# A power moved ahead of a selection, three more zero products, and K begun on the upper part of the context

## The chip, the cores and the metric

The kernel runs on one core of a Trainium2 chip. The metric is the device time of an execution in microseconds (us); before the change the median of three runs is 744.03 us. Names used: TensorE (PE), its weight loads (PEld), VectorE (DVE), ScalarE (ACT), GpSimd (POOL), SyncE (SP), which only issues DMAs.

## The reference

For 32 batches of `x` and `ctx`, each 64 channels by 512 positions, in float32:

```python
q, k, v = layernorm(x), ctx, ctx
qh, kh, vh = Wq q, Wk k, Wv v              # 8 heads of 64 channels, 512 positions
qh = softmax(qh, over channels) / 8 ; kh = softmax(kh, over positions)
context = kh vh^T ; out = context^T qh ; out = Wo out + bo
x = x + out / max(norm(out, over channels), 1e-12) * g * 8

xf = layernorm(x)                          # 2048 rows of 512
inter = xf c1^T c2^T                       # 1792 columns, 56 blocks of 32
idx = argmax in each block
h = relu(w1[idx] . xf)                     # one of 32 per block
x = x + sum over blocks of h * w2t[idx]
```

## The kernel before

One program covers both halves. Each engine has its own list of instructions, written out by hand as functions; their order on an engine is the order of the calls, and between engines they wait for each other by semaphore counts. Float32 operands of the products are split into an upper part (`_hi`, `_high`) and a rest (`_lo`, `_low`), so that a product is three terms: upper by upper, and twice upper by rest.

**The attention** takes one batch per step, `step(g, ...)` for g from -1 to 33. On TensorE a step has `keys(0)`, `keys(1)` (K's two halves, line 1300, into `slot[0]` and `slot[1]`), the products with V (line 1274) and with Q (line 1277) of the batches before, `queries(0)`, `queries(1)` (line 1314, into the same slots) and transposes of E and Q. VectorE takes the maxima (`max_k` line 784, `max_q` line 750) and shifts Q (`shift_q`, line 759); ScalarE takes the exponentials and copies.

The **start** is the step g = -1 and the step g = 0. On TensorE the step -1 is `zeros(12)`: products of a tile of zeros (line 1214), into a bank that nothing reads. On SyncE `ctx[0]` is loaded first. ScalarE rounds it into `c_high[0]` (line 1022, counts `c_hi`), VectorE subtracts into `c_low[0]` (line 804, counts `c_ready`). `keys(0)` waits for `c_ready` and for `wk_lo`. The terms of `keys` go n = 0, 1, 2: (`wk_hi`, `c_high`), (`wk_lo`, `c_high`), (`wk_hi`, `c_low`), two products each. In step 0 `keys(1)` is followed by `fold_vo()` (line 1075, waits for `wv` and `woT`), `zeros(4)`, a wait for small loads, `queries(0)`, `zeros(5)`, `queries(1)`, which waits for the exponential of K's second half. VectorE in that time: `split_wk`, `c_low`, `statistics(0)` (lines 767 and 769), `max_k(0)`, `split_first_x` (lines 773 to 778; its last, `x_low`, is what `queries(0)` waits for), `max_k(1)`, `max_q(0)`, `shift_q(0)`, `statistics(1)`, `max_q(1)`, `shift_q(1)`.

**The second half** takes rows in pairs of 128-row tiles ("duos", d = 0 to 7). A duo has 8 uses, u = 0 to 7: four chunks of `inter`'s columns (256, 512, 512, 512 wide; u // 2 is the chunk) by two tiles (u % 2). For one use: `project(d, u)` on TensorE (line 1129); `block_max(d, u)` on VectorE (lines 640 and 645: block maxima, and a mask of the places that reach them); `rank_mask(d, u)` on GpSimd (line 451); `first_max(d, u)` on VectorE (line 653); `select(d, u)` on GpSimd (line 464, writes `behind`); and then on SyncE the transposes of `behind`, 128 by 128 each (`turn_mask`, line 293: two for a use of the first chunk, four for the others). Seven pairs of 128 hidden columns, i = 0 to 6, use the transposed masks: `hide(d, i)` on TensorE (line 1147, 24 products), `gate(d, i)` on VectorE (line 663; for i = 1 and 2 it waits for the transposes of u = 2 and u = 3, so twelve in all stand ahead of `gate(0, 1)`), `h_high(d, i)` on ScalarE (line 928), `h_low(d, i)` on VectorE (line 669), `down(d, i)` on TensorE (line 1165, 12 products, waits for `h_low(d, i)`).

In the same duo the next two tiles, a = 2d + 2 and a + 1, are prepared: `norms(a)` on VectorE (lines 596 and 598: sums of squares per channel group, into `norm`), `invert(a, 2)` on GpSimd (line 423: their power -1/2, for both tiles), `turn_factors(a, 2)` on TensorE (line 1097, waits for `invert`), `exchange(d)` on ScalarE (line 886 copies the factors, line 892 stores them, line 898 issues four DMAs that load them spread over the channels), `scale` (line 602), `residual` (609), `moments_of` (614, 616) and `normalize` (621) on VectorE with `prepare` on GpSimd (408, 412) between, and `turn_x(a)`, `turn_x(a + 1)` on TensorE (line 1106).

The order around the change in the first pair is, on TensorE from `duo(0)`: `hide(0, 1)`, `turn_factors(2, 2)`, `project(0, 6)`, `hide(0, 2)`, `down(0, 0)`, `project(0, 7)`, `down(0, 1)`, `hide(0, 3)`, `turn_x(2)`, `turn_x(3)`, `hide(0, 4)`. On VectorE: `first_max(0, 2)`, `norms(2)`, `norms(3)`, `block_max(0, 4)`, `gate(0, 0)`, and from `duo(0)`: `first_max(0, 3)`, `h_low(0, 0)`, `first_max(0, 4)`, `block_max(0, 5)`, `first_max(0, 5)`, `gate(0, 1)`, `block_max(0, 6)`, `h_low(0, 1)`, `gate(0, 2)`, then `scale`, `residual` and `moments_of` for both tiles and `normalize(2)`, `first_max(0, 6)`, `normalize(3)`. On GpSimd: `select(0, 2)`, `rank_mask(0, 4)`, and from `duo(0)`: `select(0, 3)`, `invert(2, 2)`, `rank_mask(0, 5)`, `select(0, 4)`, `select(0, 5)`, `rank_mask(0, 6)`, `prepare(2)`, `prepare(3)`.

Of the kernel before, what the change touches and what calls it, by code (L numbers as in the profile page):

```python
# [81 lines left out]
def program(nc, A, scratch, factors, out):  # L82
    with ExitStack() as ctx:
# [150 lines left out]
        with nc.Block() as block:  # L234
# [164 lines left out]
            def _(pool):  # L399
# [19 lines left out]
                def invert(a, w):  # L419
                    pool.wait_ge(norm_max, a + w)  # L420
                    if a > 1:
                        pool.wait_ge(inv_turned, a // 2 + 1)
                    nc.gpsimd.tensor_tensor(inv[:, a % 2:a % 2 + w], norm[:, a % 2:a % 2 + w],
                                            neg_half[:].unsqueeze(2).broadcast_to([P, w, 2 * NT]),
                                            ALU.pow).then_inc(norm_inv, 1)
# [18 lines left out]
                def rank_mask(d, u):  # L444
                    use, w = USES * d + u, CHUNKS[u // 2][1]
                    if use == 0:
                        pool.wait_ge(rank_done, 1)
                    pool.wait_ge(i_mask, use + 1)
                    if later(use - 1):
                        pool.wait_ge(i_sel, use - 1)  # L450
                    nc.gpsimd.tensor_tensor(blocks(ranked[u % 2][:, 0:w]), blocks(mask[u % 2][:, 0:w]),  # L451
                                            rank[:].unsqueeze(1).broadcast_to([P, w // SPARSE, SPARSE]),
                                            ALU.mult).then_inc(i_ranked, 1)

                def select(d, u):
                    use, w = USES * d + u, CHUNKS[u // 2][1]
                    pool.wait_ge(i_first, use + 1)
                    if use in (0, 2):
                        pool.wait_ge(q_turned, HT * (B - 1 + use // 2))
                    if u >= 4:  # L460
                        pool.wait_ge(mask_in[u - 4], 16 * (CHUNKS[(u - 4) // 2][1] // P) * (d + 1))
                    elif later(d):
                        pool.wait_ge(mask_in[u + 4], 16 * (CHUNKS[(u + 4) // 2][1] // P) * d)
                    nc.gpsimd.tensor_tensor(blocks(behind[use % 4][:, 0:w]), blocks(ranked[u % 2][:, 0:w]),  # L464
                                            spread(first[u % 2][:, 0:w // SPARSE], w // SPARSE),
                                            ALU.subtract).then_inc(i_sel, 1)

                def duo(d, last):
                    select(d, 3)
                    if not last:  # L470
                        invert(2 * d + 2, 2)
                    rank_mask(d, 5)
                    select(d, 4)
                    select(d, 5)
                    rank_mask(d, 6)
                    if not last:
                        prepare(2 * d + 2)
                        prepare(2 * d + 3)
                    select(d, 6)
                    rank_mask(d, 7)  # L480
                    select(d, 7)
                    if not last:
                        begin(d + 1)

                def begin(d):
                    rank_mask(d, 0)
                    rank_mask(d, 1)
                    select(d, 0)
                    rank_mask(d, 2)
                    select(d, 1)  # L490
                    rank_mask(d, 3)
                    select(d, 2)
                    rank_mask(d, 4)

                def step(g, k, par, known):
# [87 lines left out]
            def _(dve):  # L583
# [7 lines left out]
                def norms(a, bank):  # L591
                    t = a % 2
                    dve.wait_ge(squared, a + 1)
                    if later(a - 1):
                        dve.wait_ge(norm_inv, inverted(a - 2))
                    nc.vector.tensor_reduce(by_factor(norm[:, t]), by_pair(bank[:]), AX.X, ALU.add).then_inc(norm_sum, 1)
                    dve.wait_ge(norm_sum, a + 1)
                    nc.vector.tensor_scalar(norm[:, t], norm[:, t], NORM_EPS * NORM_EPS, None, ALU.max).then_inc(norm_max, 1)
# [49 lines left out]
                def first_max(d, u):  # L648
                    use, w = USES * d + u, CHUNKS[u // 2][1]
                    dve.wait_ge(i_ranked, use + 1)  # L650
                    if later(use - 1):
                        dve.wait_ge(i_sel, use - 1)
                    nc.vector.tensor_reduce(first[u % 2][:, 0:w // SPARSE], blocks(ranked[u % 2][:, 0:w]), AX.X,  # L653
                                            ALU.max).then_inc(i_first, 1)
# [23 lines left out]

                def duo(d, last):
                    a = 2 * d + 2  # L680
                    first_max(d, 3)
                    h_low(d, 0)
                    first_max(d, 4)
                    block_max(d, 5)
                    first_max(d, 5)
                    if d:
                        result_of(2 * d - 2)
                        result_of(2 * d - 1)
                    gate(d, 1)
                    block_max(d, 6)  # L690
                    h_low(d, 1)
                    gate(d, 2)
                    if not last:
                        for t in range(2):
                            scale(a + t)
                            residual(a + t)
                            moments_of(a + t)
                        normalize(a)
                    first_max(d, 6)
                    if not last:  # L700
                        normalize(a + 1)
                    block_max(d, 7)
                    if not last:
                        xT_rest(a, pre[0])
                        xT_rest(a + 1, pre[1])
                    h_low(d, 2)
                    first_max(d, 7)
                    gate(d, 3)
                    gate(d, 4)
                    if not last:  # L710
                        z_low(d + 1)
                    h_low(d, 3)
                    if not last:
                        block_max(d + 1, 0)
                        block_max(d + 1, 1)
                        first_max(d + 1, 0)
                    h_low(d, 4)
                    if not last:
                        block_max(d + 1, 2)
                        first_max(d + 1, 1)  # L720
                        block_max(d + 1, 3)
                    gate(d, 5)
                    if not last:
                        first_max(d + 1, 2)
                    gate(d, 6)
                    if not last:
                        block_max(d + 1, 4)
                    if d + 2 < DUOS:
                        norms(a + 2, pre[0])
                    h_low(d, 5)  # L730
                    if d + 2 < DUOS:
                        norms(a + 3, pre[1])
                    h_low(d, 6)
                    if not last:
                        gate(d + 1, 0)
# [125 lines left out]
                first_max(0, 2)  # L861
                norms(2, pre[0])
                norms(3, pre[1])
                block_max(0, 4)
                gate(0, 0)
                duos(duo)
# [204 lines left out]
            def _(pe):  # L1071
# [144 lines left out]
                def step(g, k, par, known):  # L1216
                    if known == -1:
                        pe.wait_ge(idle_set, 1)
                        zeros(12)
                        return  # L1220

                    def turn_e(m):
# [66 lines left out]
                    def keys(s):  # L1289
                        if real(known, 0):  # L1290
                            if s == 0:
                                pe.wait_ge(c_ready, g + 1)
                                pe.wait_ge(wk_lo_done, 1)
                            if later(2 * g - 1 + s):
                                pe.wait_ge(q_shifted, 2 * g - 1 + s)
                            for n, (w, c) in enumerate(((wk_hi, c_high), (wk_lo, c_high), (wk_hi, c_low))):
                                for i in range(2):
                                    j = slice((2 * s + i) * P, (2 * s + i + 1) * P)
                                    rows = slice(i * C, (i + 1) * C)
                                    last = nc.tensor.matmul(slot[s][:, i, :], w[rows, j], c[par][rows, :],  # L1300
                                                            start=(n == 0), stop=(n == 2))
                            last.then_inc(k_proj, 1)
# [107 lines left out]
```

## Time and profile before

| | us |
|---|---|
| timed runs | 744.03 median of 744.01, 744.03, 745.66 |
| the profiled execution | 745.32 |
| its span | 743.5 |
| TensorE busy | 731.8 (98% of the span) |
| VectorE busy | 624.0 (84%) |
| GpSimd busy | 494.5 (67%) |
| ScalarE busy | 401.3 (54%) |

The span is what the profile covers; the execution's own time has 1.8 us around it. The attention takes the first 380 us or so; the second half's first pair stands at about 383 to 425 us. The granted clock of TensorE is given as a share of 2.4 GHz, so 0.5 is 1.2 GHz.

### The profile page before, as it was taken

Reading aid. Unit: us, or ns where it says so; the run is one execution under the profiler, and the core shown is the slowest. Engines: PE = TensorE matmul, PEld = TensorE weight load, DVE = VectorE, ACT = ScalarE, POOL = GpSimd, SP = SyncE. Lnnn points to the kernel's source line nnn. Section 1 sums busy time; section 2 is a strip of 40 time slices with the busy share of each in tenths; the row PEclk is TensorE's granted clock in tenths of the full one; section 3 lists DMA queues with packets and bytes.
Section 4 is the critical chain, followed back from the end, with each engine's and each line's share of the span. In section 5 each row is a group of like instructions: output and inputs, shape, how many; then the busy total and the mean of one; then the engine's idle time right before and its main releaser. Section 6 shows DMA issues by size and latency. Waiting matters only on the chain.

```text
span 743.5 us, 14542 instructions
## 1 busy us (share of the span) xinstructions
PE 731.8 (98%) x5155; PEld 556.8 (75%) x5155; DVE 624.0 (84%) x908; ACT 401.3 (54%) x780; POOL 494.5 (67%) x512
## 2 busy tenths in 40 slices
PE   8999999999999999999998999999999999999998
PEld 6566665665665665656667889899898988989896
DVE  6999999999999999999977878787777887778642
ACT  4899999999999999999841111112111111211110
POOL 2789999999998888778756554544545354554420
PEclk9999999999999999999999999999999999999999
DMA  7224434344333332322123224141231414121110
GB/s 170 64 74 121 112 105 122 98 111 129 100 97 101 92 110 73 100 66 78 23 72 62 79 35 123 22 132 25 53 104 35 123 21 107 51 52 49 25 52 30
DMA packets 69191, 59.47 MB, mean 80 GB/s; under 512 B 41344, under 2 KB 50304, under 8 KB 69120
## 3 DMA queue, kind: packets, MB, share of 16 engines
q1 hardware_dynamic: 65920, 53.98, 27.0%
q10 hardware_dynamic: 3200, 4.58, 3.0%
q8 instruction: 41, 0.67, 0.4%
q14 instruction: 30, 0.25, 0.1%
HBM read 42.71 MB, written 8.45 MB: 69 GB/s over the span
## 4 chain that ended last, share of the span: by engine, by line
PE 84%; DVE 5%; POOL 4%; issue 3%; ACT 2%; SPq 2%; DMA 1%; DVEq 0%; POOLq 0%
PE slot L1147 20%; PE po L1274 12%; PE po L1165 10%; PE turn L1165 10%; PE turn L1259 7%; PE turn L1242 6%; PE slot L1300 6%; PE slot L1314 6%; PE po L1285 2%; PE slot L1129 2%; POOL Q L561 2%; SPq L293 1%; DVE qsum L790 1%; PE turn L1106 1%; PE turn L1117 1%
## 5 line engine op out<-in xcount | busy, mean ns | idle before, releaser
L451 POOL TENSOR_TENSOR E<-E,rank 128x512 bf16<-128x512 bf16 (+1 forms) x64 | 70.1, 1096 | 106.2 <-DVE E L645 105.2
L561 POOL TENSOR_TENSOR Q<-Q,qrec 128x1024 f32<-128x1024 f32 x64 | 121.1, 1905 | 26.7 <-DVE qrec L798 26.6
L1277 PE MATMUL po<-QT,G 128*64 128x512 f32 x256 | 116.9, 599 | 0.0
L1274 PE MATMUL po<-E,ctxT 128*64 128x512 f32 x256 | 116.9, 598 | 0.0
L975 ACT ACTIVATE E<-slot,neg_kmax 128x512 f32<-128x512 f32 x128 | 86.4, 685 | 10.5 <-DVE neg_kmax L784 10.0
L750 DVE TENSOR_REDUCE qmax<-slot 128x16 f32<-128x1024 f32 x64 | 75.3, 1217 | 13.5 <-PE slot L1314 13.4
L464 POOL TENSOR_TENSOR behind<-E,first 128x512 bf16<-128x512 bf16 (+1 forms) x64 | 62.7, 985 | 33.6 <-DVE first L653 33.3
L1274 PEld LDWEIGHTS po<-E,ctxT 128*64 128x64 f32 x256 | 32.3, 136 | 64.7 <-issue 56.9
L790 DVE TENSOR_REDUCE qsum<-Q 128x16 f32<-128x1024 f32 x64 | 77.2, 1206 | 1.5 <-ACT Q L964 1.5
L784 DVE TENSOR_REDUCE neg_kmax<-slot 128x2 f32<-128x1024 f32 x64 | 76.3, 1192 | 1.0 <-PE slot L1300 0.6
L983 ACT ACTIVATE E<-turn 128x512 f32<-128x512 f32 x128 | 75.0, 612 | 3.3 <-PE turn L1242 2.5
L759 DVE TENSOR_TENSOR Q<-slot,qmax 128x1024 f32<-128x1024 f32 x64 | 75.2, 1214 | 0.1
L1242 PE MATMUL turn<-ident,E 128*128 128x128 f32 x512 | 74.6, 279 | 0.5 <-ACT E L983 0.5
L964 ACT ACTIVATE Q<-Q 128x1024 f32<-128x1024 f32 x64 | 70.1, 1096 | 3.2 <-DVE Q L759 3.2
L992 ACT ACTIVATE QT<-turn 128x512 f32<-128x512 f32 x128 | 70.3, 615 | 2.2 <-PE turn L1259 2.2
L1259 PE MATMUL turn<-ident,Q 128*128 128x128 f32 x512 | 69.8, 279 | 1.3 <-POOL Q L561 1.3
L1242 PEld LDWEIGHTS turn<-ident,E 128*128 128x128 f32 x512 | 56.0, 140 | 14.1 <-issue 11.7
L1147 PE MATMUL slot<-c_high,weights_lo 128*128 128x256 f32 x224 | 63.8, 285 | 0.0
L1147 PE MATMUL slot<-c_high,weights_hi 128*128 128x256 f32 x224 | 63.7, 285 | 0.0
L1147 PE MATMUL slot<-c_low,weights_hi 128*128 128x256 f32 x224 | 63.6, 284 | 0.0
L1147 PE MATMUL slot<-xT_hi,weights_hi 128*128 128x256 f32 x224 | 63.2, 282 | 0.0
L1147 PE MATMUL slot<-xT_hi,weights_lo 128*128 128x256 f32 x224 | 63.0, 281 | 0.0
(182 smaller groups left out, 1952.9 us busy)
## 6 DMA issues: line engine op xcount, KB each, us to landing
c_in<-in_ctx SPq DMA_DIRECT2D x64, 128.0 KB, 2.7
x_in<-in_x SPq DMA_DIRECT2D x64, 128.0 KB, 2.6
stage<-in_ffn_w SPq DMA_DIRECT2D x32, 225.0 KB, 2.5
out<-E SPq DMA_DIRECT2D x16, 256.0 KB, 2.3
ctxT<-in_ctxT SPq DMA_DIRECT2D x31, 128.0 KB, 2.1
attn_out<-po_sb SPq DMA_DIRECT2D x31, 128.0 KB, 2.3
stage<-attn_out SPq DMA_DIRECT2D x8, 256.0 KB, 4.1
E<-attn_out SPq DMA_DIRECT2D x7, 256.0 KB, 4.5
```

What stands on the lines that cost most here:

```text
L561: nc.gpsimd.tensor_tensor(half, half, qrec[1 - par][:, s, :].unsqueeze(2).broadcast_to([P, HALF, D]), ALU.mult).then_inc(q_scaled, 1)
L750: nc.vector.tensor_reduce(qmax[:, s, :], heads(slot[s][:]), AX.X, ALU.max).then_inc(q_max, 1)
L759: nc.vector.tensor_tensor(heads(Q[par][:, 2 * s:2 * s + 2, :]), heads(slot[s][:]), qmax[:, s, :].unsqueeze(2).broadcast_to([P, HALF, D]), ...
L784: nc.vector.tensor_reduce(neg_kmax[par][:, 2 * s:2 * s + 2], slot[s][:], AX.X, ALU.max, negate=True).then_inc(k_max, 1)
L790: nc.vector.tensor_reduce(qsum[:, s, :], heads(Q[q][:, 2 * s:2 * s + 2, :]), AX.X, ALU.add).then_inc(q_sum, 1)
L975: last = nc.scalar.activation(E[par][:, j, :], slot[s][:, i, :], ACT.Exp, bias=neg_kmax[par][:, j:j + 1], accum_out=ksum[par][:, j:j + 1])
L1147: last = nc.tensor.matmul(by_tile(hidden[q % 2][:, j * 2 * P:(j + 1) * 2 * P]), w, x, start=(n == 0), stop=(n == len(terms) - 1))
L1165: last = nc.tensor.matmul(acc[t][:], h[q % 3][:, cols], w2(wt, 2 * i + j), start=(i == 0 and j == 0 and n == 0), stop=(i == PAIRS_H - 1 an ...
L1242: last = nc.tensor.transpose(bank_e(g, m)[:, j * P:(j + 1) * P], E[par][:, j, m * P:(m + 1) * P], ident[:])
L1259: last = nc.tensor.transpose(bank_q(g, m)[:, t * P:(t + 1) * P], Q[1 - par][:, t, m * P:(m + 1) * P], ident[:])
L1274: nc.tensor.matmul(po[0:C, :], ctxT[1 - par][:, m, :], E[1 - par][:, :, m * P:(m + 1) * P], start=(m == 0), stop=(m == NT - 1)).then_inc(p ...
L1277: nc.tensor.matmul(po[C:P, :], G[:, m, :], QT[m][:], start=(m == 0), stop=(m == HT - 1)).then_inc(out_mm, 1)
```

## The change

In the first pair GpSimd does the power of the next two tiles behind `select(0, 2)`, then `select(0, 3)`, and only then `rank_mask(0, 4)`; VectorE does `first_max(0, 3)` behind `norms(3)`, ahead of `block_max(0, 4)`. The later pairs keep their order. In step -1 there are fifteen zero products for twelve. In step 0 K's first two terms wait for `c_hi`, and only its third for `c_ready`.

```diff
@@ gpsimd
                 def duo(d, last):
-                    select(d, 3)
-                    if not last:
-                        invert(2 * d + 2, 2)
+                    if d:
+                        select(d, 3)
+                        if not last:
+                            invert(2 * d + 2, 2)
                     rank_mask(d, 5)
...
@@ begin(d)
                     rank_mask(d, 3)
                     select(d, 2)
+                    if d == 0:
+                        invert(2, 2)
+                        select(d, 3)
                     rank_mask(d, 4)
@@ vector
                 def duo(d, last):
                     a = 2 * d + 2
-                    first_max(d, 3)
+                    if d:
+                        first_max(d, 3)
                     h_low(d, 0)
...
                 norms(2, pre[0])
                 norms(3, pre[1])
+                first_max(0, 3)
                 block_max(0, 4)
                 gate(0, 0)
                 duos(duo)
@@ tensor
                     if known == -1:
                         pe.wait_ge(idle_set, 1)
-                        zeros(12)
+                        zeros(15)
                         return
...
                             if s == 0:
-                                pe.wait_ge(c_ready, g + 1)
+                                if known == 0:
+                                    pe.wait_ge(c_hi, 1)
+                                else:
+                                    pe.wait_ge(c_ready, g + 1)
                                 pe.wait_ge(wk_lo_done, 1)
...
                             for n, (w, c) in enumerate(((wk_hi, c_high), (wk_lo, c_high), (wk_hi, c_low))):
+                                if known == 0 and s == 0 and n == 2:
+                                    pe.wait_ge(c_ready, 1)
                                 for i in range(2):
```

## Rows read from the trace of the kernel before

**Rows 1.** The page's first line

```profile
span 743.5 us, 14542 instructions
```

**Rows 2.** Waits of TensorE, 385 us to the end: total, times, longest

```profile
PE turn L1097 <- POOL inv L423: 2.4, 1, 2.4
PE turn L1106 <- DVE work L621: 0.4, 1, 0.4
```

**Rows 3.** The chain that ended last, 385 to 412 us: start, length, what

```profile
...
393.60 1.23 SPq L293
...
397.42 2.33 DMA x_in<-behind
...
409.27 1.30 DVE work L621
...
410.62 0.66 PE turn L1106 x4
```

**Rows 4.** Timeline, GpSimd and VectorE, 388 to 402 us: start, length, operation

```profile
391.77 1.04 POOL L464 TENSOR_TENSOR behind<-E,first 128x512 bf16<-128x512 bf16 x1
392.77 3.38 POOL L423 TENSOR_TENSOR inv<-norm,neg_half 128x16 f32<-128x16 f32 x1
...
389.01 0.17 DVE L598 TENSOR_SCALAR norm<-norm 128x8 f32<-128x8 f32 x1
...
401.77 0.68 DVE L669 SCALAR_TENSOR_TENSOR hT_lo<-gated,wk_lo 128x512 fp32r<-128x512 f32 x1
```

**Rows 5.** Stretches: window, length, PE busy, granted clock, DMA share, GB/s

```profile
393.80:396.20 2.40, 0.02 (x1) 1.00 0.09 18
...
397.00:400.50 3.50, 3.50 (x19) 0.51 0.27 55
```

**Rows 6.** Timeline, ScalarE's DMA issues, 398 us

```profile
398.23 1.33 ACTq L898 DMA_DIRECT2D x_in<-factors x2
```

**Rows 7.** The transposes (line 293) issued around 397.4 and around 400 us

```profile
L293 SPq DMA_TRANSPOSE x_in<-behind x2: 1233/1234/1234, 396.1 to 397.4; - x2
DMA to landing us min/median/max: 2.3/2.3/2.3
...
L293 SPq DMA_TRANSPOSE x_in<-behind x2: 1231/1234/1236, 398.7 to 400.0; - x2
DMA to landing us min/median/max: 4.6/4.6/4.7
```

**Rows 8.** A stretch of the start, columns as in rows 5

```profile
8.00:11.20 3.20, 3.20 (x20) 0.50 1.08 258
```

**Rows 9.** Timeline of the start, 1 to 15 us

```profile
1.04 4.60 PE L1214 MATMUL turn<-QT 128*128 128x128 f32 x24 [1.04 <-DVE QT L801]
...
6.29 0.63 ACT L1022 ACTIVATE c_high<-c_in 128x512 fp32r<-128x512 f32 x1 [2.88 <-DMA c_in<-in_ctx]
...
7.70 0.60 PE L1300 MATMUL slot<-c_high,wk_hi 64*128 64x512 f32 x2 [2.06 <-DVE c_low L804]
...
8.41 0.18 DVE L769 BATCH_NORM_AGGREGATE moments<-stats 128x2 f32<-128x6 f32 x1
...
9.19 1.23 DVE L784 TENSOR_REDUCE neg_kmax<-slot 128x2 f32<-128x1024 f32 x1 [0.60 <-PE slot L1300]
...
11.37 0.69 DVE L778 TENSOR_TENSOR x_low<-x_in,x_high 128x512 fp32r<-128x512 f32 x1
...
11.88 1.16 PE L1214 MATMUL turn<-QT 128*128 128x128 f32 x8
...
12.96 0.50 PE L1314 MATMUL slot<-wq_hi,x_high 64*128 64x512 f32 x2
...
13.97 1.23 DVE L750 TENSOR_REDUCE qmax<-slot 128x16 f32<-128x1024 f32 x1 [0.77 <-PE slot L1314]
```

**Rows 10.** The load of `woT` (line 300), issue and time to landing

```profile
L300 SPq DMA_DIRECT2D Q<-in_woT x1: 597/597/597, 3.9 to 3.9; - x1
DMA to landing us min/median/max: 5.0/5.0/5.0
```

## The prediction, made before the changed kernel ran

> **What bounds the kernel now.** The profiled execution took 745.32 us, a span of 743.5 us [rows 1] with 1.8 us around it; the three timed runs gave 744.03 (median), 744.01 and 745.66 us. TensorE is nearly always busy, so I ask only where it isn't, or runs at a lower clock. I read four views for that, in this order.
>
> First the waits of TensorE from 385 us to the end: there are two, 2.4 us for GpSimd's power (line 423) and 0.4 us for VectorE's `work` (line 621) [rows 2]. The first is what part one of the change is aimed at. Second the chain that ended last, over the same stretch [rows 3]. The reader is to see that the power is not on it: it goes through SyncE's mask transposes, issued one behind another, one each 1.27 us, through the landing of the twelfth (397.42 + 2.33 = 399.75), which frees `gate(0, 1)` on VectorE, and from there over VectorE and GpSimd to `normalize(3)` at 409.27 and to `turn_x(3)` on TensorE at 410.62. Behind that point the second list of waits is empty: whatever moves 410.62 moves the end by as much. Third the timeline of the start, and fourth the granted clock there.
>
> **Part one, GpSimd's order.** Now: `select(0, 3)` 391.77 to 392.81, power 392.77 to 396.15 [rows 4]. After: the power waits for `norms(3)`, done at 389.18 [rows 4], and `select(0, 2)` is done by 388.4; so it runs from 389.25 to 392.65 (3.38 us). Behind it stands `select(0, 3)`: 392.65 to 393.7. SyncE's last four transposes of the first two chunks wait for that one. SyncE was free for them and started them at 393.60 [rows 3]; now they start at about 393.74: 0.14 us late. `first_max(0, 3)` moves in front of `block_max(0, 4)` and `gate(0, 0)` on VectorE, each 0.6 us later; what waits for `gate(0, 0)` is ScalarE, which is held until 391.9 by its own DMA issue: nothing. `rank_mask(0, 4)` moves behind all this and ends at 394.9; `block_max(0, 5)` then ends at 396.9, and TensorE asks for it at 399.7: nothing.
>
> TensorE's 2.4 us are gone: `hide(0, 1)` ends at 393.8 [rows 5], and the transpose of the factors, which waited 2.4 us, follows at once; with its pipelining I take 2.5 us. The granted clock was 0.51 from 397.0 to 400.5, behind this idle stretch [rows 5]: `hide(0, 2)` ran there on the 1.2 GHz level, and at 2.4 GHz it saves 1.6 us more. So `hide(0, 2)`, `down(0, 0)` and `project(0, 7)` end at 399.9 for 403.96. Next is `down(0, 1)`, which waits for `h_low(0, 1)`, and that stands behind `gate(0, 1)` on VectorE: 401.77 + 0.68 = 402.45 [rows 4]. The 4 us that TensorE gains have nowhere to go.
>
> Now what the earlier factors set off. ScalarE stores them and issues four broadcast loads (line 898) from 398.23 on [rows 6]. Two transposes issued before these loads landed in 2.3 us each; the two issued 0.5 and 1.7 us behind the first load took 4.7 and 4.6 us [rows 7]. In the kernel before all twelve of `gate(0, 1)` had been issued by then, the last at 397.42. After, the loads begin at 398.23 - 2.5 = 395.7, and the last two of the twelve, at 396.3 and 397.5, stand 0.6 and 1.8 us behind, in just the place of the slow pair. The last lands at 397.5 + 4.65 = 402.2 for 399.75: **2.45 us late**. VectorE is in order, so `block_max(0, 6)`, `h_low(0, 1)`, the residuals, moments and `normalize(3)` all move by this; on SyncE only transposes of later chunks are behind. `turn_x(3)` comes at 413.07.
>
> Bounds: if the twelfth lands in 2.3 us the delay is 0.14. It can't be a gain, since the transposes' chain from 383.2 on isn't shortened by anything. Upward: TensorE would wait for `h_low(0, 1)` from 399.9 to 404.9. Behind idle stretches of 2.4 and 2.1 us the clock was at 0.5 for 3.5 and 3.2 us [rows 5, 8, 9], so it will fall here too. From 404.9 it has `down(0, 1)`, `hide(0, 3)` and `turn_x(2)` to do, 6.25 us at full clock: 411.15, 1.9 us ahead of 413.07. With 3.5 us at the lower level (1.75 us lost) the delay is hidden; with twice that it is 1.6 us more. So part one costs 0.14 to 4.0 us, and I take 2.45.
>
> A rule of the Trainium skill speaks to the same place. The page DMA: Bandwidth & Descriptors, section Issuing engines are not separate DMA queues, says that DMAs issued by different engines run on the same 16 DMA engines and interleave; by that rule the trace's slow pair is no accident. The same page, section Anatomy of one DMA, gives a DMA a fixed cost of about 2.0 us and then its bytes; by that alone the twelfth would land as before, and the sum would be rival (a)'s.
>
> **Part two, the start.** Now twelve zero products (24 records) end at 5.64, and K begins at 7.70, on `c_low` [rows 9]. The clock is at 0.50 from 8.0 to 11.2 [rows 8], behind the 2.06 us without work. Three more products are 6 records, at most 0.145 us each (8 took 1.16) [rows 9]: 0.9 us, an end at 6.5 at the latest. K's first two terms need only `c_high`, ready at 6.92, and `wk_lo`, ready before that: K begins at 6.97. The idle stretch falls from 2.06 to 0.5 us. What it does between the two no row shows; 0.5 is far from the 2.1 and 2.4 that cost the clock, so I take it as kept.
>
> K's third term can't start before 7.70, when `c_low` is there; at full clock a pair of such products takes 0.50, as Q's do at 12.96 [rows 9], so K's first half is done at 8.2 for 9.15. VectorE is then the next limit: its moments end at 8.59, so `max_k(0)` starts at 8.55 for 9.19, 0.64 us earlier, and so is `x_low`, ready at 11.42 for 12.06. ScalarE's exponential moves with it. TensorE stood at this place behind its own slow work: K, the folding of V and O and four zero products kept it until 12.96 [rows 9]. At full clock K ends at 8.75; the folding waits for `woT`, landing at 3.9 + 5.0 = 8.9 [rows 10], and takes at most 1.6, its time now, at the lower clock; with the zeros done by 11.4. Q's first half then starts at 11.48 for 12.96. VectorE has `max_k(1)`, moved too, until 12.57, so `max_q(0)` starts at 12.49 for 13.97: **1.48 us earlier**. From there VectorE runs without a gap to 19.7, Q's second half (it waits for the exponential of K's second half, 14.1) is there before 15.7, and everything behind moves by 1.48. The next context tile, landed at 12.3 and split at 14.28, is wanted at 17.2: hidden. The other loads are issued on counts that move along.
>
> Bounds: if the clock falls all the same, K's third term still ends in time for VectorE, but TensorE reaches Q only 0.65 us earlier. So the start gives 0.65 to 1.5 us against the profiled execution.
>
> **The sum.** Against the profiled execution: 745.32 - 1.48 + 2.45 = 746.3 us. It was 1.3 us above the median, though, and one timed run was 1.6 us above. The cost of the slow K is of this size (1.48, less the 0.25 that an early start gives at full clock): the two faster runs may have had it at full clock already. I can't tell from one trace. If so, the start gives the median 0.25 us; if not, 1.48. Halfway: 0.87. Forecast 744.03 - 0.87 + 2.45 = **745.6 us**, +0.2%. About 0.3%, 2.2 us, is what a measurement of this kernel can tell from no change.
>
> **Rivals.** (a) The transposes land in 2.3 us beside the loads; part one costs 0.14, the start gives its 0.25 to 1.48: 742.7 to 743.9 us. For it: the slow pair is one place, and more transposes stood behind it in SyncE's queue; against it: nothing else differs between the pairs. Chance 0.25. The fixed cost of the Trainium skill's page DMA: Bandwidth & Descriptors would give the same. (b) Slower: the lower clock behind the 5 us wait for `h_low(0, 1)` stays for twice the 3.5 us shown. Then TensorE and not `normalize(3)` sets `turn_x(3)`: 4.0 - 0.25 to 1.48, so 746.6 to 747.8 us. It decides from 1.9 us of lost work on. Chance 0.15. (c) The fifteen products don't keep the clock up: start 0.65 for 1.48, and the median near 744.03 - 0.65 + 2.45 = 745.8. Chance 0.1. The forecast itself, with the start's gain anywhere between its ends (745.0 to 746.25): 0.5.
>
> Faster than 741.8 would need a gain in the first pair that I exclude: 0.03. Slower than 746.26 takes (b) and the edge of the forecast: 0.22. Within: 0.75. The range 742.8 to 747.2 leaves out the outer ends of (a) and (b).
>
> **What would show it.** Right: K's first product near 6.97 at clock 1.0; Q's first at 11.5; `max_q(0)` at 12.5; in the first pair (times less 1.5) no wait at line 1097, but one of about 5 us at line 1165 for line 669, the clock at 0.5 behind it, and the landing of the last transpose ahead of `gate(0, 1)` at 4 to 5 us. Wrong: a landing at 2.3 us and `turn_x(3)` 1.3 us earlier than 410.62; or K still at 0.5.

## The result, and the profile after

Each kernel was timed in alternation with the kernel before.

| | before | after |
|---|---|---|
| median, us (14 runs each) | 744.15 (743.2 to 746.7) | 745.75 (744.7 to 746.64) |
| ratio after / before | | 1.002, 95% interval 1.0011 to 1.0029 |
| the profiled execution, us | 745.32 | 744.74 |
| its span, us | 743.5 | 742.9 |

The change makes the kernel 0.2% slower, 1.6 us by the medians; the interval leaves out 1. The profiled executions stand the other way round: the one of before is over its median, the one of after near the bottom of its runs. So the traces show where time moves, and the timed runs how much it is worth.

The waits of TensorE from 385 us to the end, after (kind of wait: total, times, longest). In [rows 2] there were two, on the power and on `work`; the one on the power is gone, and one on `h_low` has come. (`stage` and `work` are what `normalize(2)` and `normalize(3)` write. The changed kernel and the kernels of the experiments have more lines than before's, so the same line has a somewhat higher number in their views.)

```profile
PE po L1171 <- DVE hT_lo L673: 3.8, 1, 3.8
PE turn L1112 <- DVE work L625: 0.7, 2, 0.5
```

The chain that ended last, after, answering to [rows 3] (start, length, what; `select` and the first transposes ahead of it, then the pieces up to `turn_x(3)`):

```profile
383.58 1.09 SPq L293
...
391.09 1.23 SPq L293
...
394.92 3.68 DMA x_in<-behind
...
398.68 0.10 DVE gated L667
...
408.12 1.31 DVE work L625
...
409.47 0.66 PE turn L1112 x4
```

The same pieces as before, with one changed: the landing of the last transpose ahead of `gate(0, 1)` took 3.68 us for 2.33. In before the piece that answers to 383.58 stood at 386.09, and from there to `turn_x(3)` it was 24.53 us; here it is 25.89. The difference is 1.36, the landing's is 1.35. The lower clock behind TensorE's wait is not in it: TensorE stands and waits 0.3 us for `work` right ahead of `turn_x(3)`, so it was there in time even so.

The last transpose itself, and ScalarE's DMA issues of the loads and GpSimd's power in the timeline after, answering to [rows 4, 6, 7]:

```profile
L293 SPq DMA_TRANSPOSE x_in<-behind x1: 1232/1232/1232, 394.9 to 394.9; - x1
...
DMA to landing us min/median/max: 3.7/3.7/3.7
```

```profile
386.76 2.93 POOL L423 TENSOR_TENSOR inv<-norm,neg_half 128x16 f32<-128x16 f32 x1 [0.91 <-DVE norm L602]
389.66 1.04 POOL L464 TENSOR_TENSOR behind<-E,first 128x512 bf16<-128x512 bf16 x1
...
393.13 1.38 ACTq L904 DMA_DIRECT2D x_in<-factors  x2
```

The first load is issued at 393.13, and the transpose at 394.92, 1.8 us behind. Fourth, TensorE's clock around its wait (window, length, PE busy, granted clock, DMA share, GB/s):

```profile
397.30:401.30 4.00, 0.20 (x1) 1.00 0.18 40
...
401.50:404.70 3.20, 3.20 (x8) 0.50 0.13 26
```

And the start, answering to [rows 9]:

```profile
1.04 5.74 PE L1220 MATMUL turn<-QT 128*128 128x128 f32 x30 [1.04 <-DVE QT L806]
...
6.96 0.49 PE L1311 MATMUL slot<-c_high,wk_hi 64*128 64x512 f32 x2 [0.19 <-ACT c_high L1028]
...
7.69 0.50 PE L1311 MATMUL slot<-c_low,wk_hi 64*128 64x512 f32 x2
...
8.59 1.19 DVE L789 TENSOR_REDUCE neg_kmax<-slot 128x2 f32<-128x1024 f32 x1
...
11.53 0.50 PE L1325 MATMUL slot<-wq_hi,x_high 64*128 64x512 f32 x2 [0.26 <-DVE x_low L783]
...
12.53 1.23 DVE L755 TENSOR_REDUCE qmax<-slot 128x16 f32<-128x1024 f32 x1
```

The fifteen zero products end at 6.78, K begins at 6.96, its third term waits for `c_low` until 7.69, and `max_q(0)` comes at 12.53 for 13.97.

### The profile page after: what moved, and what is told of

It is laid out like the page before. It is cut to its first block, busy times and chain, and to the rows that moved or that the text cites. A ratio compares the mean times of both kernels' runs of the same rounds, so it can differ in the third digit from the quotient of the medians.

```text
span 742.9 us, 14554 instructions
## 1 busy us (share of the span) xinstructions
PE 731.2 (98%) x5161; PEld 556.6 (75%) x5161; DVE 622.3 (84%) x908; ACT 401.1 (54%) x780; POOL 493.8 (66%) x512
## 4 chain that ended last, share of the span: by engine, by line
PE 86%; POOL 3%; DVE 2%; ACT 2%; DMA 2%; issue 2%; SPq 2%; POOLq 0%; DVEq 0%
PE slot L1153 19%; PE po L1280 13%; PE po L1171 10%; PE turn L1171 10%; PE turn L1265 8%; PE turn L1248 7%; PE slot L1311 6%; PE slot L1325 6%; PE po L1291 2%; PE slot L1135 2%; SPq L293 1%; POOL Q L565 1%; PE turn L1112 1%; PE turn L1123 1%; PE turn L1096 1%
```

## The experiments

Theory 1 is the prediction's: part one loses because the factors' loads, begun earlier, slow the landing of the transposes ahead of `gate(0, 1)`; part two gains, but only where K would have run at half clock. Its rivals: the loss comes from the start, or from TensorE's wait and the lower clock behind it.

**First, the two parts and the halves of part two, each alone.** `e1_order_only` is the changed kernel with the start of before, `e2_start_only` the kernel before with the new start. `e3_zeros_only` and `e4_upper_only` split the start (here and below, lines left out of a diff stand as `...`, or stand between its parts):

```diff
# e3_zeros_only, against before
-                        zeros(12)
+                        zeros(15)
# e4_upper_only, against before
-                                pe.wait_ge(c_ready, g + 1)
+                                if known == 0:
+                                    pe.wait_ge(c_hi, 1)
+                                else:
+                                    pe.wait_ge(c_ready, g + 1)
...
+                                if known == 0 and s == 0 and n == 2:
+                                    pe.wait_ge(c_ready, 1)
```

> Part one alone (GpSimd's power ahead of the fourth selection, first_max(0, 3) earlier); the start is as before. Theory 1, the landing: the factors' loads start some 2.5 us earlier and catch the last transposes ahead of gate(0, 1), which land in 3.7 to 4.7 us for 2.3; no wait of TensorE for line 423, one of about 4 us for h_low(0, 1) instead, clock at 0.5 behind it; 1.3 to 2.5 us slower than before (ratio 1.0017 to 1.0034). Rival, the order is harmless and the change's loss comes from the start: within 0.4 us of before (1.0000 to 1.0005).

> Part two alone (fifteen zero products and K's first terms on the upper part); the first pair is as before. Theory 1: K begins at 6.97 us at full clock, max_q(0) at 12.5; TensorE's wait of 2.4 us for line 423 stays; faster than before by something between 0.25 us (if most runs of before have K at full clock already) and 1.48 us: ratio 0.998 to 0.9997. Rival, the loss comes from the start (what is moved earlier there meets the loads of the attention worse): slower than before by 0.5 us or more.

> Fifteen zero products alone, K still waits for its rest. Theory 1: K begins at 7.70 at full clock, its first half is done at 8.7, so max_k(0) at 8.75 for 9.19 and max_q(0) near 12.7 for 13.97: against the profiled execution 1.2 us less, against the median 0 to 1.2 us (ratio 0.9984 to 1.0000). If the clock falls all the same: 13.97 less 0 to 0.2.

> K's first terms on the upper part alone, twelve zero products. The idle stretch ahead of K is 5.64 to 6.97, 1.3 us, between the 0.2 that kept the clock and the 2.06 that lost it. If the clock is kept: as e2, max_q(0) at 12.5. If it falls: max_k(0) at 8.55, but TensorE reaches Q only 0.65 us earlier than before, max_q(0) at 13.3, ratio 0.9991.

| | median, us | ratio to before (95%) |
|---|---|---|
| e1, order only | 745.19 | 1.0022 (1.0013 to 1.003) |
| e2, start only | 743.86 | 0.9998 (0.9987 to 1.0008) |
| e3, zeros only | 744.22 | 1.0002 (0.9993 to 1.0011) |
| e4, upper part only | 743.05 | 0.9992 (0.9983 to 1.0001) |
| before, beside them | 743.65 | |

Part one alone makes the whole loss, and part two is worth nothing that these runs can tell from zero; nor are its halves. The rival that puts the loss at the start falls. In e1's chain the landing is long again:

```profile
396.23 3.71 DMA x_in<-behind
...
410.80 0.66 PE turn L1112 x4
```

The start of e1 is a surprise worth having: its instructions are those of before, yet K ran at full clock. Its first product of K, and the next pair, in the timeline:

```profile
7.53 0.50 PE L1306 MATMUL slot<-c_high,wk_hi 64*128 64x512 f32 x2 [1.00 <-DVE c_low L809]
7.87 0.40 PE L1306 MATMUL slot<-c_high,wk_lo 64*128 64x512 f32 x2
```

and its `max_q(0)` came at 12.52. TensorE had been idle for 1.0 us there, where it was 2.06 in before's trace: K began 0.17 us earlier, and above all the twelve zero products took 5.49 us, for 4.60 in before. In e4, with twelve products too, it was 1.08 us idle and K at full clock; in e3 the rest of the context came late (K at 7.83, 1.64 us idle) and the clock was kept as well. e2 has K at 7.22 and `max_q(0)` at 12.80, each some 0.3 us behind what was expected: its context came later too.

**Second, the cause of part one's loss.** `e5_loads_later` holds the loads back until the last of those transposes is issued. `e8_warm_wait` keeps TensorE at work in its wait. `e6_tile2_first` moves work of VectorE into the hole that the late landing leaves, and `e7_tile2_warm` is e6 with e8's products. All four start from the changed kernel:

```diff
# e5_loads_later, in exchange(d) on ScalarE
+                    if d == 0:
+                        act.wait_ge(i_ranked, 6)
                     for t in range(2):
                         for b in range(2):
                             nc.scalar.dma_start(spread_of(a + t)[b * C:(b + 1) * C, :], over_channels(a + t, b))\
# e8_warm_wait (and e7), on TensorE
                     project(d, 7)
+                    if d == 0:
+                        for _ in range(14):
+                            nc.tensor.matmul(pre[1][:, 0:P], ident[:], ident[:], start=True, stop=True)
                     down(d, 1)
# e6_tile2_first (and e7), on VectorE
+                    else:
+                        scale(a)
+                        residual(a)
+                        moments_of(a)
                     gate(d, 1)
...
-                        for t in range(2):
+                        for t in range(0 if d else 1, 2):
```

> The changed kernel, but in the first pair ScalarE's four loads of the factors wait until GpSimd has done rank_mask(0, 5), so they start about 0.7 us behind the issue of the last transpose ahead of gate(0, 1), and not 1.8 us ahead of it. Theory 1, the landing: that transpose lands in 2.3 us again, turn_x(3) comes 1.35 us earlier after the first transpose (24.5 us for 25.9), and the loss of part one is gone: within 0.5 us of before (ratio 0.9993 to 1.0007). Rival, the loss comes from TensorE's idle stretch and its lower clock: both are still there (2.4 us and more), so still 1.3 us or more slower (1.0017 and up).

> The changed kernel with the same fourteen products alone. Theory 1: the clock stays at 1.0 through the wait, but turn_x(3) waits for normalize(3), so nothing is gained where the lower clock's 1.7 us are hidden: ratio to before 1.0015 to 1.0030, as the changed kernel. Rival (b) of the prediction, the lower clock sets the loss: 0.5 to 1.6 us faster than the changed kernel (1.0000 to 1.0013).

> The changed kernel, with scale, residual and moments of tile 2 in the first pair moved ahead of gate(0, 1) on VectorE, into the 2.4 us in which it waits for the transposes. The loads are early enough for it now. VectorE's chain to normalize(3) gets about 2 us shorter, gate(0, 1) 0.6 us later; then TensorE itself, at the lower clock behind its wait, sets turn_x(3): within 0.7 us of the changed kernel, so 0.9 to 2.3 us slower than before (1.0012 to 1.0031). If the lower clock costs nothing here: turn_x(3) 1.2 us earlier than in the changed kernel.

> As e6, and fourteen products of the identity behind project(0, 7) (some 3.0 us, nothing reads them) that keep TensorE busy in its wait for h_low(0, 1). Theory 1: the clock stays at 1.0, TensorE reaches turn_x(2) some 1.6 us earlier than in e6, turn_x(3) 1.0 to 1.4 us earlier than in the changed kernel: within 0.7 us of before (0.9990 to 1.0010). If the transposes ahead of gate(0, 1) land even later: as e6.

| | median, us | ratio to before (95%) |
|---|---|---|
| e5, loads later | 743.73 | 0.9999 (0.9985 to 1.0012) |
| e8, work in the wait | 745.32 | 1.0018 (1.0006 to 1.003) |
| e6, tile 2 first | 746.76 | 1.0035 (1.002 to 1.0051) |
| e7, tile 2 first and work in the wait | 745.17 | 1.0015 (1.0 to 1.0029) |
| before, beside them | 743.77 | |

e5 takes the loss away with one wait. Its chain, and with it ScalarE's issue of the loads:

```profile
394.67 2.34 DMA x_in<-behind
...
408.03 0.66 PE turn L1114 x4
```

```profile
395.45 1.38 ACTq L906 DMA_DIRECT2D x_in<-factors  x2
```

The first load is issued 0.8 us behind the last transpose, and that one lands in 2.34 us; the DMA records have the load's first large packet at 397.02, when the transpose has just landed (397.01). TensorE still waits 2.6 us for `h_low(0, 1)` in this kernel, so the wait as such is not what costs. But the clock stayed at 1.00 behind it (400 to 403 us), against what was expected: e5 takes the long landing and the lower clock away together, and e8 has to tell them apart.

e8 puts the same question to the clock. The fourteen products hold it at 1.00 throughout:

```profile
397.00:401.00 4.00, 4.00 (x32) 1.00 0.60 67
401.00:403.00 2.00, 0.28 (x2) 1.00 0.10 21
403.00:409.00 6.00, 5.79 (x37) 1.00 0.14 27
```

and the time stays that of the changed kernel (1.0018 for 1.002): the loss is there without the lower clock, and TensorE only waits longer for `normalize(3)` (1.3 us in e8's waits). But it is not a clean trade, since this trace also has a landing 1.0 us longer than the changed kernel's:

```profile
395.33 4.70 DMA x_in<-behind
...
410.89 0.66 PE turn L1112 x4
```

A landing of 4.70 and one of 3.68 differ in one thing that the profile shows. While the transpose of e8 is under way, 395.33 to 400.03, a load of instructions runs on the same DMA engines; in the changed kernel, 394.92 to 398.60, none does. From the DMA view of both stretches (queue, kind: packets, MB, share of 16 engines; e8, then after):

```profile
q10 hardware_dynamic: 299, 0.48, 60.0%
q1 hardware_dynamic: 477, 0.10, 12.9%
q8 instruction: 1, 0.02, 1.6%
```

```profile
q10 hardware_dynamic: 301, 0.49, 46.5%
q1 hardware_dynamic: 480, 0.10, 16.8%
```

It is a packet of 16 KB at 396.62 in e8 and at 396.21 in e7 (landing 4.70), where the fourteen products are; in after, e1 and e6 it comes at 402.6 or later, behind the landing of 3.7 to 3.9. No experiment moved this packet alone, so that it is the cause of the last 1 us is not shown; the fourteen products may well be what brings it forward.

Put side by side, the distance from the transpose that answers to 386.09 in before to `turn_x(3)`, and the landing, from the chains of ten profiled executions:

| kernel | landing, us | transpose to `turn_x(3)`, us |
|---|---|---|
| before; twice more (b1, b2, below) | 2.33; 2.34, 2.34 | 24.53; 24.60, 24.55 |
| e2 | 2.35 | 24.56 (383.90 to 408.46) |
| e3; e4 | 2.34; 2.34 | 24.55; 24.56 |
| e5 | 2.34 | 24.69 (383.34 to 408.03) |
| after | 3.68 | 25.89 |
| e1 | 3.71 | 25.91 (384.89 to 410.80) |
| e8 | 4.70 | 26.89 (384.00 to 410.89) |

The difference of the two columns is 22.2 to 22.35 us in all ten, with the clock behind TensorE's wait at 0.50 (after) and at 1.00 (e5, e8): apart from the landing the way to `turn_x(3)` is the same in all of them. This excludes the clock better than e8's time does. The timed runs of e8 say less than its trace: 2.37 us of landing would be a ratio of 1.0032, and measured is 1.0018, at most 1.003. The landing is also long in e6 (3.9 us) and e7 (4.7), whose chains don't go through it.

e6 missed its expectation on the bad side: 1.0035, where at most 1.0031 was expected for it. `scale(2)` itself has to wait for its factors, which land at 397.26, so the work does not fit into the hole. With tile 2 ahead of it `gate(0, 1)` comes later (400.34, for 398.68 in after), TensorE waits 5.3 us for `h_low(0, 1)`, and its products behind that run at half clock:

```profile
403.00:406.00 3.00, 2.99 (x7) 0.50 0.13 27
406.00:408.40 2.40, 2.40 (x8) 0.54 0.15 31
```

Here TensorE is late for `turn_x(2)` and `turn_x(3)`, so the clock counts. e7 differs only by the fourteen products and is 1.6 us faster by the medians (745.17 for 746.76); it missed its expectation (1.0010 at most) by a little, since the clock fell there later, behind the 2.2 us that it still waits (0.72 over 403 to 409 us). The lower clock is real, then, and in e6 it is the likely cost, since its products are all that e7 changes; in the change it is hidden.

**Third, a version of its own, and the start once more.** Only the first two transposes of u = 2 and u = 3 hold what `gate(0, 1)` reads. `e10_halves_before` counts each use's transposes in two halves, with before's order and e4's start; `e9_halves` does it with the changed order and e4's start, and with `gate(0, 1)` ahead of `first_max(0, 5)`, `h_low(0, 1)` ahead of `block_max(0, 6)` and `gate(0, 2)` behind the moments in the first pair. `b1_before_again` and `b2_before_again` are the kernel before.

```diff
# e9_halves and e10_halves_before
+        mask_hi = [sem(f"mask_hi{u}") for u in range(USES)]
...
-                            .then_inc(mask_in[u], 16)
+                            .then_inc((mask_in, mask_hi)[i // 2][u], 16)
...
-                        dve.wait_ge(mask_in[u], 16 * (CHUNKS[c][1] // P) * (d + 1))
+                        dve.wait_ge((mask_in if i == 0 or i % 2 else mask_hi)[u], 32 * (d + 1))
...
```

The part left out has `select` on GpSimd wait for both halves.

> A version of its own: the changed kernel's order with twelve zero products, and the transposes of each use of four counted in two halves on semaphores of their own, so that gate(0, 1) waits only for the first two of u = 2 and u = 3, which are all that it reads; the last two, which meet the loads, are waited for by gate(0, 2), and in the first pair that gate stands behind the moments of both tiles, with h_low(0, 1) ahead of block_max(0, 6). Theory 1: gate(0, 1) comes about 2.5 us sooner after the first transpose than in before, the early loads now serve scale(2), and turn_x(3) comes some 22.6 us after the first transpose for 24.5: 1 to 2.5 us faster than before (ratio 0.9966 to 0.9987). Rival, VectorE or the loads bind in its place: within 0.5 us.

> The two halves alone, in the order of before (the power late, the loads late), with K's first terms on the upper part. Theory 1: gate(0, 1) is early, but gate(0, 2) and then scale(2), whose loads are still issued late, hold VectorE: turn_x(3) at most 0.4 us earlier after the first transpose than before, ratio 0.998 to 1.0000. So the two parts of e9 need each other.

> The kernel before, unchanged, for one more look at its start. Is K at half clock in each execution, or in some? If in some: K at full clock and max_q(0) near 12.5 to 12.7 us, or K at half clock and max_q(0) near 14.0, with an execution 1.2 to 1.5 us longer in the second case.

> The same once more: K at full clock or at half clock, max_q(0) near 12.6 or 14.0 us.

e9 gave 743.64 us beside 743.42, ratio 0.9998 (0.9987 to 1.0009): the gain that I expected is not there, and the rival's "within 0.5 us" is. `turn_x(3)` comes 23.65 us after the first transpose (383.97 to 407.62), 0.9 us sooner than in before, where 22.6 was expected. Its chain goes through ScalarE, whose issues of the four early loads (393.54 to 396.20) now stand in front of `h_high(0, 1)`, and then over VectorE. TensorE waits 2.1 us for `stage` in front of `turn_x(2)`, and behind that the clock falls, in front of work that nothing hides:

```profile
405.00:407.50 2.50, 0.66 (x4) 0.98 0.14 30
407.50:411.00 3.50, 3.38 (x17) 0.53 0.50 157
```

e10 gave **742.68 us, ratio 0.9988 (0.998 to 0.9997)**, the only version that is faster than the kernel before beyond its interval, and faster than the changed one. I had expected 0.998 to 1.0000, and `turn_x(3)` at most 0.4 us earlier: it comes 24.08 us after the first transpose (383.84 to 407.92), about 0.5 earlier. Its only wait of TensorE in this half is the old one, on the power:

```profile
PE turn L1101 <- POOL inv L424: 2.4, 1, 2.4
```

and now this wait is on the chain that ended last, not VectorE as I had expected. The power, and TensorE behind it at half clock (0.57 over 394.5 to 398.0):

```profile
390.57 3.35 POOL inv L424
...
394.70 4.14 PE slot L1151 x24
```

So the power that the change moved first may be worth moving once the transposes are off the chain; e9 moved both and met the loads' issues instead, and no run here shows a version that gains by it. How much of e10's gain is the halves and how much K's early start (0.9992 alone in e4) the intervals don't separate.

b1 (742.96 us) and b2 (743.26 us) both have K at full clock, behind 1.32 and 1.18 us without work, and `max_q(0)` at 12.07 and 12.03. From b1's timeline:

```profile
7.08 0.51 PE L1300 MATMUL slot<-c_high,wk_hi 64*128 64x512 f32 x2 [1.32 <-DVE c_low L804]
...
12.07 1.23 DVE L750 TENSOR_REDUCE qmax<-slot 128x16 f32<-128x1024 f32 x1
```

So of four profiled executions with the old start (before, e1, b1, b2) one had K at half clock, the one in which TensorE was idle longest, 2.06 us: its zero products ended first (5.64 us, for 5.76, 5.88 and 6.53) and its K began last (7.70, for 7.08, 7.06 and 7.53).

## Why the prediction was right

**The forecast** was 745.6 us from a median of 744.03; measured 745.75 beside 744.15. The loss was called 1.6 us and is 1.6 by the medians. It is smaller than the 2.2 us that the prediction called tellable, but the interval lies wholly above 1, and e1 repeats it. The mechanism of part one is right; that the number is met so exactly is luck, since two terms were too large and cancel (below).

**Part one, mechanism: right.** The wait on the power goes, TensorE's gain has nowhere to go, the loads begin 2.5 us earlier against the transposes and catch the last one, VectorE's chain moves by as much (1.36 for 1.35 us), and `turn_x(3)` with it. e5 takes the loss away by issuing the loads later, e1 and e2 exclude the start, and the clock is excluded by TensorE's own wait for `work` ahead of `turn_x(3)`, by e8, where the loss is there at full clock, and by the table above.

**Part one, size: 2.45 was too much; it is 1.36.** The term is the landing, taken as 4.65 us from two neighbouring transposes of before [rows 7]. It was 3.7 in after and e1. The prediction held that nothing else differs between the fast and the slow pair of before; that reading was wrong. Before's DMA records have two loads of instructions beside the slow pair, 8 KB at 401.85 and 16 KB at 404.15, and none beside the fast one. From the DMA view of 398.70 to 403.36, while the first of the slow pair is under way:

```profile
q14 instruction: 1, 0.01, 0.5%
```

The slow pair is no accident of one execution: it takes 4.5 to 4.8 us in all six executions whose first pair is that of before (before, b1, b2, e2, e3, e4), and each has such a load beside it. In the place where the change puts the twelfth transpose there is none, and it took 3.7 to 3.9 (after, e1, e6). Whether the instructions are the cause was not tried, but the price was read from a place that had more beside it than the place it was used for. By the timed runs part one is 1.6 us (e1, 0.0022 of 744), whose interval, 1.0 to 2.2 us, holds the 1.38 of e1's landing and leaves out 2.45. The 0.14 us of a late start of the transposes never came: the power took 2.93 us there, for 3.38 in before, and SyncE went on without a gap (391.09).

**Rival (a)**, a landing of 2.3 us, is refuted by all six executions with the early loads (after, e1, e6, e7, e8, e9: 3.7 to 4.7 us). The fixed cost that the Trainium skill gives (DMA: Bandwidth & Descriptors, section Anatomy of one DMA), there for DMAs issued by GpSimd and by the prediction taken over to SyncE's, does not hold beside the loads. The traces agree with what the Trainium skill says of the sharing of DMA engines (DMA: Bandwidth & Descriptors, section Issuing engines are not separate DMA queues): 2.33 us for a transpose issued ahead of the loads, 3.7 to 4.7 for one issued 1.8 us behind the first. **Rival (b)**, the lower clock: it came, at 0.50 from 401.5 to 404.7, but for 3.2 us only, and hidden, as the bound of 1.9 us of lost work said: TensorE still had 0.3 us to wait for `work`. TensorE waited 3.8 us and not the 5.0 forecast, by the shorter landing. **Rival (c)**, fifteen products that don't keep the clock: none of the executions with them showed it.

**Part two, against the profiled execution: right.** K at 6.96 for a forecast of 6.97, Q's first half at 11.53 for 11.48, `max_q(0)` at 12.53 for 12.49: 1.44 us earlier, forecast 1.48. Two small slips are in it. `max_k(0)` was put at 8.55, ahead of the end of VectorE's moments, which the same paragraph has at 8.59; it came at 8.59, and the 0.04 us runs through. And a zero product was taken at 0.145 us, from eight that took 1.16; by [rows 9] the 24 records at the start took 0.19 each, so fifteen end at 6.78 and not at 6.5 at the latest. That left 0.19 us idle ahead of K instead of 0.5, and did no harm here.

**Part two, against the median: the step that I halved should not have been halved.** I took 0.87 us, halfway between 0.25 (the median run has K at full clock already) and 1.48 (it doesn't). The first is the case in three of four profiles, and e2 measures 0.9998. From the moment `c_low` is ready, `max_q(0)` comes 4.99 us later in b1 (7.08 to 12.07) and 4.84 in after (7.69 to 12.53): the early start is worth 0.15 us, and the three more zero products can at best save an execution in which the context comes late; e3's profiled execution was such a one (K at 7.83) and kept the clock, which is one case and no proof. That half was too large by some 0.7 us, and the landing too large by 1.1 (2.45 for 1.36; 0.8 against e1's timed runs). The two errors go opposite ways and nearly cancel in the sum, which is why it came so close. This is luck.

Between the start and the first pair, and behind it, the two traces differ by about 1 us and 0.6 us for no reason of the change. Behind it, after has one wait of 0.5 us more, for `work` in a later pair (between 580 and 640 us); e2 and e3, whose first pair is that of before, have it too (0.6 and 0.5 us). From a `keys(0)` of the attention to the same transpose it is 106.18 us in before (279.91 to 386.09), 105.31 in after, and 105.38, 106.44 and 105.77 in e2, e3 and e4, whichever edit they have. What moves there was not followed further.

## What to carry to other kernels

Before you remove a wait of the busiest engine, look whether it stands on the chain that ends last, and if it doesn't, ask what the earlier work will start: here a 2.4 us wait off the chain bought nothing, and the loads released early made a transfer on the chain land 1.35 us later, 2.4 in e8. Issue the transfer that others wait for ahead of the less urgent ones; one wait on the less urgent transfer (e5) restores that. When you take a price from one place of a trace, compare all that runs beside it with the place where you use it, loads of instructions too. And profile a start more than once: a saving read from one trace may be the price of that one execution.

## What the runs showed of the hardware

- The landing of a DMA transpose depends on what runs beside it. The twelfth took 2.33 to 2.35 us in seven executions (before, b1, b2, e2, e3, e4, e5), in which the first load was issued 0.8 to 0.9 us behind it, and 2.75 in e10, where an 8 KB load of instructions ran beside it. Issued 1.8 us or so behind the first of four broadcast loads of 128 KB, on another engine's queue, it took 3.7, 3.7 and 3.9 us (after, e1, e6), and 4.4, 4.7 and 4.7 where a load of instructions ran beside it as well (e9, e7, e8).
- A load's packets come well behind its issue: issued at 398.23 in before, its first large packet stands at 399.70; 393.13 and 394.67 in after.
- The granted clock fell to 0.5 behind idle stretches of 2.06 and 2.4 us (before), 3.8 us (after), 5.3 us (e6) and 2.1 us (e9); it was kept behind 1.0 (e1), 1.08 (e4), 1.18 (b2), 1.32 (b1) and 1.64 us (e3). But it was also kept behind 2.6 us in e5 and behind the 2.4 us of the same wait on the power in e2, so the length of one idle stretch alone doesn't decide it.
- The same power of 128 x 16 elements on GpSimd took 2.93 or 2.94 us in the first pair of all executions with the changed order (after, e1, e5 to e9), and 3.38 in that of the others, with different work of VectorE beside it. Why was not tried.
